# Causal attention of a decoder layer in four strips of 32 queries instead of two of 64

## What is computed

```
q, k, v = proj(Wq), proj(Wk), proj(Wv)           # (B, 16, 128, 8), of layernorm(x)
qn, kn = sum(q*q), sum(k*k);  qk = q @ k.T
ed = sqrt(max(qn - 2 qk + kn, 0) + 1e-8);  ns = qn + kn
dist = where(ed < 0.1, ed*(1 + c*ns/2 + c*c*ns*ns/8),
             where(ed > 2, 0.693 + log(ed + 1e-8) + c*ns/4, ed*sqrt(1 + c*ns)))
scores = where(key <= query, -beta*dist, -inf)
x = x + (softmax(scores) @ v) @ Wo.T
```

## Time and profile before

| | before |
|---|---|
| device time, median of 3 runs | 266.76 us (265.5 to 267.89) |
| span of the profiled execution | 263.8 us |
| what lies around the span, taken as median less span | 3.0 us |
| busy PE, DVE, ACT, POOL | 209.1, 202.4, 168.2, 119.4 us |
| mean granted TensorE clock, as a share of full speed | 0.830 |

### The profile page before, as it was taken

How to read it: one execution, slowest core, us unless ns; L and a number is a source line. 1 busy time by engine, 2 the same in 40 slices (tenths; PEclk the granted TensorE clock), 3 DMA queues, 4 the chain that set the end, 5 groups by cost and what they waited for, 6 DMA issues and landing times. The chain is left out here.

```text
span 263.8 us, 4889 instructions
## 1 busy us (share of the span) xinstructions
PE 209.1 (79%) x1588; PEld 165.1 (63%) x1589; DVE 202.4 (77%) x515; ACT 168.2 (64%) x329; POOL 119.4 (45%) x153
## 2 busy tenths in 40 slices
PE   0695442678795997589799886789999999899995
PEld 0243131566674786468566653267888788789884
DVE  5867979999999999997866479966577843855554
ACT  2499889999999999794247421358355567433320
POOL 5331262775666666555428106202076755735000
PEclk9997555587689559755569968999999999999999
DMA  4505776944295059300000400000000000100001
GB/s 127 148 0 157 146 209 156 262 93 85 49 295 150 2 128 346 92 1 0 2 1 2 159 0 1 0 2 0 0 2 1 1 2 0 41 2 0 0 2 40
DMA packets 35865, 17.86 MB, mean 68 GB/s; under 512 B 18680, under 2 KB 33536, under 8 KB 35584
## 3 DMA queue, kind: packets, MB, share of 16 engines
q1 hardware_dynamic: 35840, 17.54, 25.3%
HBM read 12.56 MB, written 4.98 MB: 66 GB/s over the span
## 5 line engine op out<-in xcount | busy, mean ns | idle before, releaser
L1288 DVE SCALAR_TENSOR_TENSOR dist_mem<-P,gub,dist_mem 128x512 f32<-128x512 f32 x32 | 23.8, 749 | 24.4 <-ACT dist_mem L844 24.1
L844 ACT ACTIVATE dist_mem<-P,gub 128x512 f32<-128x512 f32 x32 | 21.9, 687 | 30.8 <-PE P L1327 30.8
L583 POOL TENSOR_SCALAR m_gt<-dist_mem 128x768 uint8<-128x768 f32 x16 | 34.3, 2143 | 7.1 <-issue 5.2
L574 POOL TENSOR_TENSOR dist<-dist,cf 128x128 f32<-128x128 f32 x32 | 14.6, 457 | 40.6 <-DVE dist L1046 40.6
L1327 PE MATMUL P<-cf,dist 128*128 128x128 f32 x96 | 25.8, 356 | 6.9 <-ACT shift L772 6.9
L1327 PEld LDWEIGHTS PO<-proj_mem,dist_mem 128*128 128x128 f32 x244 | 29.4, 192 | 1.0
L1327 PE MATMUL PO<-proj_mem,dist_mem 128*128 128x128 f32 x244 | 30.0, 276 | 0.0
L1327 PE MATMUL P<-xhi,whi 128*128 128x512 f32 x64 | 26.6, 415 | 1.1 <-DVE dist_mem L1288 1.1
L1327 PEld LDWEIGHTS P<-cf,dist 128*128 128x128 f32 x96 | 17.3, 181 | 12.7 <-ACT shift L772 9.8
L1327 PE MATMUL P<-xhi,wlo 128*128 128x512 f32 x64 | 25.1, 392 | 0.0
L1327 PE MATMUL P<-xlo,whi 128*128 128x512 f32 x64 | 25.0, 390 | 0.0
(11 more groups left out here) (249 smaller groups left out, 538.7 us busy)
## 6 DMA issues: line engine op xcount, KB each, us to landing
q_split<-split_mem SPq DMA_DIRECT2D x16, 128.0 KB, 2.7
k_split<-split_mem SPq DMA_DIRECT2D x4, 512.0 KB, 3.7
stq<-q_split SPq DMA_DIRECT2D x16, 128.0 KB
stk<-k_split SPq DMA_DIRECT2D x16, 128.0 KB
split_mem<-no_rows SPq DMA_DIRECT2D x1, 1024.0 KB, 5.8
wgu<-gate_w SPq DMA_DIRECT2D x1, 1024.0 KB, 6.6
wgu<-up_w SPq DMA_DIRECT2D x1, 1024.0 KB, 9.4
dist<-no_rows SPq DMA_DIRECT2D x1, 1024.0 KB, 4.7
```

Of the source, the lines that this page charges most:

```text
L574: pool.tensor_tensor(wideq, wideq, cm, ALU.add)
L583: pool.tensor_scalar(m_gt[:, g.k % 2, :], e2[:, g.k % 2, :], 4.0 - ATT_EPS, None, ALU.is_gt).then_inc(sm["gt_done"], 1)
L844: A(sil[:, f, :], (P1, P2)[f][:, 0, :], ACT.Silu, bias=gub[:, 0, one:one + 1]).then_inc(sm["sil_done"], 1)
L1288: V.scalar_tensor_tensor(hT[:, z % 2 * 2 + f, :], (P1, P2)[f][:, 1, :], gub[:, 1, one:one + 1], sil[:, f, :], ALU.add, ALU.mult).then_inc( ...
```

## The change

The queries of a unit are cut into strips of 32. A strip s needs 32(s+1) keys, so the columns are 2 x (128 + 96 + 64 + 32) = 640 where they were 768. The partitions now hold four groups g of 32 queries (one for each head pair), and j, the head of the pair, lies in the columns. Each elementwise instruction takes 640 columns.

```diff
-UW = 768
+UW = 640
+ST = S // 4
...
+
+BLOCKS = (((3, 0, 128),), ((3, 1, 128),), ((2, 0, 96), (0, 0, 32)), ((2, 1, 96), (0, 1, 32)), ((1, 0, 64), (1, 1, 64)))
+
+
+def strip_of(t, strip):
+
+    if strip == 3:
+        return t[:, 0:256].rearrange("p (j n) -> p j n", j=2)
+    if strip == 1:
+        return t[:, 512:640].rearrange("p (j n) -> p j n", j=2)
+    two = t[:, 256:512].rearrange("p (j n) -> p j n", j=2)
+    return two[:, :, 0:96] if strip == 2 else two[:, :, 96:128]
+
 
 LN_SHIFT = float(np.exp(2 * (0.693 - 0.25)))
```

```diff
-                keys = bl * S
-                for g in range(4):
-                    i, j = g // 2, g % 2
-                    q = [sq_[k][:, (g * PB + bl) * 2 + m].rearrange("p h t -> p (h t)") for m in range(2)]
-                    mm(P[:, i, j * S:(j + 1) * S], q[1], right[k][:, g, keys:keys + S])
-                    last = mm(P[:, i, 2 * S + j * HALF:2 * S + (j + 1) * HALF], q[0], right[k][:, g, keys:keys + HALF])
+                for strip in (3, 2, 1, 0):
+                    for g in range(4):
+                        q = sq_[k][:, g, bl * S + strip * ST:bl * S + (strip + 1) * ST]
+                        keys = right[k][:, g * PB + bl, :, 0:(strip + 1) * ST]
+                        last = mm(strip_of(P[g * ST:(g + 1) * ST, :], strip), q, keys)
                 last.then_inc(sm[done], 1)
```

```diff
@@ -1417,23 +1443,18 @@
                     if o is not None:
                         wait(pe, "o_copied", o)
                     out_ = PO[:, bl * 144:(bl + 1) * 144]
-                    for i in range(2):
-                        for j in range(2):
-                            for h in range(2):
-                                head = 2 * (4 * k + 2 * i + j) + h
-                                hl = 2 * (2 * i + j) + h
-                                w = pT[:, t.k % 2, i * 384 + j * S + h * HALF:i * 384 + j * S + (h + 1) * HALF]
-                                mm(out_[HALF:128, head * 9:head * 9 + 9], w, vab[:, b, k, hl * 9:hl * 9 + 9])
-                        for h in range(2):
-                            w = pT[:, t.k % 2, i * 384 + 2 * S + h * HALF:i * 384 + 2 * S + (h + 1) * HALF]
-                            first = 2 * (4 * k + 2 * i) + h
-                            dst = out_[0:HALF, first * 9:first * 9 + 36].rearrange("p (q n) -> p q n", n=18)[:, :, 0:9] \
-                                if first * 9 + 36 <= 144 else None
-                            if dst is None:
-                                dst = out_[0:HALF, (first - 1) * 9:(first - 1) * 9 + 36].rearrange(
-                                    "p (q n) -> p q n", n=18)[:, :, 9:18]
-                            c0 = 72 + 36 * i + 18 * h
-                            last = mm(dst, w, vab[:, b, k, c0:c0 + 18].rearrange("p (q n) -> p q n", q=2))
+                    for g in range(4):
+                        for n in (0, 2, 4, 1, 3):
+                            w = pT[:, t.k % 2, n * S + g * ST:n * S + (g + 1) * ST]
+                            first = 2 * (4 * k + g)
+                            if n == 4:
+                                last = mm(out_[ST:2 * ST, first * 9:first * 9 + 18], w, vab[:, b, k, 3, g * 18:(g + 1) * 18])
+                                continue
+                            for strip, j, _ in BLOCKS[n]:
+                                of = {3: 0, 2: 1, 0: 2}[strip]
+                                at_ = (first + j) * 9
+                                last = mm(out_[strip * ST:(strip + 1) * ST, at_:at_ + 9], w,
+                                          vab[:, b, k, of, (2 * g + j) * 9:(2 * g + j + 1) * 9])
                     last.then_inc(sm["pv_done"], 1)
                 at(k_, 3)
```

The transposes are five with their five shift products instead of six and six. The row minima are four reductions instead of two:

```diff
+                    m = nm[:, low.k % 2, 0, :].rearrange("p (s j) -> p s j", j=2)
+                    for strip in (3, 2, 1, 0):
+                        last = V.tensor_reduce(m[:, strip, :], strip_of(d, strip), AX.X, ALU.min, negate=True)
+                    last.then_inc(sm["nm0_done"], 1)
```

GpSimd's causal additions: three, of 128, 64 and 64 columns, instead of four of 128. It also clears a `vab` of twice the size and both stn at the start, and fills two of the forms of v:

```diff
+                pool.memset(sn_[k][:, :, :, :].rearrange("p g j t -> p (g j t)").bitcast(fp32), 0.0).then_inc(sm["zeroed_n"], 1)
+            link(pool.memset(vab[:, :, :, :, :], 0.0))
+            for k in range(2):
+                v4 = [vab[:, :, k, n, :].rearrange("p b (h n) -> p b h n", n=DH + 1) for n in range(4)]
+                link(pool.memset(v4[0][:, :, :, DH], 1.0))
+                link(pool.memset(v4[1][0:96, :, :, DH], 1.0))
+                link(pool.memset(v4[2][96:128, :, :, DH], 1.0))
+                link(pool.memset(v4[3][0:HALF, :, 0:8:2, DH], 1.0))
+                link(pool.memset(v4[3][HALF:128, :, 1:8:2, DH], 1.0))
...
+                    pool.tensor_tensor(ends, ends, cm.unsqueeze(1).unsqueeze(1).broadcast_to([128, 2, 2, ST]), ALU.add)
+                    for strip in (3, 1):
+                        end = strip_of(row, strip)[:, :, strip * ST:(strip + 1) * ST]
+                        last = pool.tensor_tensor(end, end, cm2, ALU.add)
...
+            def spread(c):
+
+                pool.wait_ge(sm["v_done"], c + 1)
+                rows = slice(c * CB, (c + 1) * CB)
+                for k in range(2):
+                    v4 = [vab[:, rows, k, n, :].rearrange("p b (h n) -> p b h n", n=DH + 1) for n in range(4)]
+                    pool.tensor_copy(v4[1][0:96, :, :, 0:DH], v4[0][0:96, :, :, 0:DH])
+                    last = pool.tensor_copy(v4[3][0:HALF, :, 0:8:2, 0:DH], v4[0][0:HALF, :, 0:8:2, 0:DH])
+                last.then_inc(sm["v_spread"], 1)
+
             for s in range(-1, NU + 1):
                 step(At(None, s))
+                if s in (0, 2):
+                    spread(s // 2)
```

The head: ACT makes six copies of v a chunk instead of ten; PE has four more products of 32 weight columns a chunk (queries of the last 32 rows for PO[96:128]), and v_full comes after them. The 256 KB that two DMAs read for stn become four small ones, after the clearing:

```diff
                 act.wait_ge(sm["v_full"], c + 1)
                 act.wait_ge(sm["init_done"], 2)
                 for k in range(2):
-                    va = vab[:, c * CB:(c + 1) * CB, k, 0:72].rearrange("p b (h n) -> p b h n", n=DH + 1)
-                    A(va[:, :, :, 0:DH], P3[:, 0, :].rearrange("p (b k h n) -> p b k h n", b=CB, k=2, h=8)[:, :, k, :, :],
+                    v4 = [vab[:, c * CB:(c + 1) * CB, k, n, :].rearrange("p b (h n) -> p b h n", n=DH + 1) for n in range(4)]
+                    A(v4[0][:, :, :, 0:DH], P3[:, 0, :].rearrange("p (b k h n) -> p b k h n", b=CB, k=2, h=8)[:, :, k, :, :],
                       ACT.Copy)
-                    for i in range(2):
-                        vb = vab[:, c * CB:(c + 1) * CB, k, 72 + 36 * i:108 + 36 * i].rearrange(
-                            "p b (j q n) -> p b j q n", j=2, q=2)
-                        lo = P3[0:HALF, 0, :].rearrange("p (b m q j n) -> p b m q j n", b=CB, m=4, q=2, j=2)
-                        hi = P3[HALF:128, 1, 0:256].rearrange("p (b m j n) -> p b m j n", b=CB, m=4, j=2)
-                        A(vb[0:HALF, :, :, 0, 0:DH], lo[:, :, 2 * k + i, 0, :, :], ACT.Copy)
-                        last = A(vb[HALF:128, :, :, 1, 0:DH], hi[:, :, 2 * k + i, :, :], ACT.Copy)
+                    A(v4[2][96:128, :, :, 0:DH],
+                      PO[96:128, :].rearrange("p (b k h n) -> p b k h n", b=CB, k=2, h=8)[:, :, k, :, :], ACT.Copy)
+                    last = A(v4[3][HALF:128, :, 1:8:2, 0:DH],
+                             P3[HALF:128, 1, 0:256].rearrange("p (b k h n) -> p b k h n", b=CB, k=2, h=4)[:, :, k, :, :], ACT.Copy)
                 last.then_inc(sm["v_done"], 1)
...
                 for b in range(CB):
-                    last = mm(P3[HALF:128, 1, b * 64:(b + 1) * 64], tok(xT, c, b)[:, 0:HALF], others)
-                last.then_inc(sm["v_full"], 1)
+                    mm(P3[HALF:128, 1, b * 64:(b + 1) * 64], tok(xT, c, b)[:, 0:HALF], others)
                 wait(pe, "wn_done", 2 * c)
                 for s in range(2):
                     pe.wait_ge(sm["sq_done"], 2 * c + s + 1)
                     mm(P2[:, s, :], headblk, qk_sq[:, s, :]).then_inc(sm["nrm_full"], 1)
+                for b in range(CB):
+                    last = mm(PO[96:128, b * S:(b + 1) * S], tok(xT, c, b)[:, 0:ST], wv_sb[:, :])
+                last.then_inc(sm["v_full"], 1)
```

```diff
-            for k in range(2):
-                sp.dma_start(sn_[k][:, :, :], stack_init).then_inc(sm["stack0"], 16)
...
-            sp.wait_ge(sm["stack0"], 32)
+            sp.wait_ge(sm["zeroed_n"], 2)
+            for k in range(2):
+                for j in range(2):
+                    ones = slice(j * HALF + 6 * DH + 3, j * HALF + 6 * DH + 6)
+                    sp.dma_start(sn_[k][ones, :, j, :], stack_init).then_inc(sm["stack0"], 16)
+            sp.wait_ge(sm["stack0"], 64)
```

The zeros that keep two heads apart move from stq to stk and stn, and with them the short runs of the loads:

```diff
-                q = q_dram[n, 2 * j + k].rearrange("a s d g (m t) -> (a s d) (g m) t", t=HALF)
-                sp.dma_start(sq_[k][half[j], :, j, :], q).then_inc(stack_in[k], 16)
+                q = q_dram[n, 2 * j + k].rearrange("a s d g t -> (a s d) (g t)")
+                sp.dma_start(sq_[k][half[j], :, :].rearrange("p g t -> p (g t)"), q).then_inc(stack_in[k], 16)
             if first:
                 sp.wait_ge(sm["k0_stored"], 16)
             for j in range(2):
```

(3 more changed lines are left out.)

## The result

The changed kernel takes 256.64 us (median of 4 runs, 255.2 to 258.33) beside 266.86 us for the kernel before (4 runs, 265.5 to 267.89): ratio 0.963, 95% interval 0.959 to 0.967, 10.2 us less. I had forecast 259.3. Its profiled execution took 257.91 us, on the longer side of the four, and spans 256.1 us, 7.7 less than before's, which by its length belongs to that kernel's shortest run (265.5). That is why the spans differ by less than the medians. The mean granted clock is 0.833, where before has 0.830, so it is not the clock that makes the difference.

A forecast was written before the change was run, and what follows sets the result against it. DVE and ACT were taken as full, PE nearly so at half clock. Loop -6.9, two later units -1.0, tail +1.2 and head -0.8 summed to -7.5, from 266.8 to 259.3 us; range 254 to 267.

The follow-up runs named there:

- one_column_group: The changed kernel with all sixteen products of a score call writing to the same 32 partitions, one column group: 259.6 us, ratio 0.975.
- pv_one_group: The changed kernel with all 28 PV products of a unit writing to the same 32 partitions, one column group: 275.8 us, ratio 1.035.
- paced: The changed kernel with stack loads in 2 KB runs, SyncE's load and wait reordered, and zeros, context and experts' weights issued apart: 252.4 us, ratio 0.946.
- group_by_group: The changed kernel with each column group's four score products issued together, instead of the four groups in turn: 256.7 us, ratio 0.962.

## What to carry to other kernels

Where small products lie in different column groups of PE, count the busiest group's weight or moving columns, not the instructions; the order in which the score products are written mattered little here. When a loop's steps get shorter, lay every issue of the DMA queue beside the new time of need, before the gain is booked: here one step took back 3.2 of 8 us, and moving one load and one wait gave them back. If a stall that was removed comes back one step later, look for the next wait in the same queue.

## What was not expected of the hardware

- Four column groups of 32 ran fully side by side, with 9 ns from one PV instruction to the next over the burst at full clock (0.51 us for 56).
- The clock did not follow PE's busy time. In one_column_group PE is busy 21.07 of 27 us and is granted 1.00; in pv_one_group it is busy 25.57 of 27 and is granted 0.50. What decides between them these runs do not settle.
- A burst of matmuls can stop for 1.2 to 5.3 us without a semaphore, at a place fixed in the program. With twice the PV instructions the stops were longer (5.06 and 5.25 us after 1.84). With spaced transfers they were shorter or, in paced, gone. PE went on 1.3 to 1.6 us after the end of an instruction packet each time.
- Products of different column groups do not start in the order of the program: in group_by_group the second group's first product starts 14 ns after the first group's, and the first group's second one 170 ns after it.
- Small instructions of VectorE took 0.2 to 0.4 us longer beside GpSimd's copies of v; why, these runs do not show.
